# The opening of a two-layer attention kernel: who splits the first projections, who issues the first queries, and where three loads stand

## The reference

```python
# layer 0: causal self-attention plus attention to a context, 16 heads of 16 channels
q, k, v    = heads(xn @ Wq + bq), heads(xn @ Wk + bk), heads(xn @ Wv + bv)        # "s"
y          = softmax(causal(q k' / 4)) v
qc, kc, vc = heads(xn @ Wcq + bcq), heads(ctx @ Wck + bck), heads(ctx @ Wcv + bcv)  # "x"
x = x + (y + softmax(qc kc' / 4) vc) @ Wp + bp          # xn = layernorm(x)
x = x + bitlinear_ffn(layernorm(x))                      # weights rounded to -1, 0, 1
# layer 1: attention to the context ("f"), then an FFN with 8-bit weights and tokens
x = x + softmax(q k' / 4) v @ Wo + bo
x = x + int8_ffn(layernorm(x))
```

## Time and profile before

| | us |
|---|---|
| median of 3 runs | 1824.35 (1822.88 to 1830.0) |
| the profiled execution, its own time | 1824.27 |
| its span, from the first to the last instruction | 1822.5 |
| busy: PE 1643.0, DVE 1356.4, ACT 1151.3, POOL 663.0 | |
| mean granted TensorE clock | 0.953 of full speed |

### The profile page before, as it was taken

The page is one execution under the profiler, slowest core; times in us unless marked ns, Lnnn a source line. Parts: engine busy times, 40 slices in busy tenths (PEclk is TensorE's granted clock), DMA queues, the critical chain, the costliest instruction groups (busy, mean ns, idle before and its releaser), DMA issues.

```text
span 1822.5 us, 29171 instructions
## 1 busy us (share of the span) xinstructions
PE 1643.0 (90%) x10064; PEld 735.4 (40%) x10064; DVE 1356.4 (74%) x2549; ACT 1151.3 (63%) x2178; POOL 663.0 (36%) x915
## 2 busy tenths in 40 slices
PE   5898799998999999998999899998999988899677
PEld 1344345433543345433543344333544443333236
DVE  6667867788687877777777868877487687687287
ACT  1474585666665686667655675657655854765497
POOL 3435323551454134532454135523561242310140
PEclk7899999999999999999999999999999997999899
DMA  7444313323142323332242324233232231123123
GB/s 193 127 113 123 81 36 100 88 82 88 55 116 71 94 66 102 88 103 59 81 107 77 87 60 111 73 103 87 77 105 51 61 98 44 44 83 133 47 70 117
DMA packets 106947, 159.49 MB, mean 88 GB/s; under 512 B 20656, under 2 KB 83248, under 8 KB 106800
## 3 DMA queue, kind: packets, MB, share of 16 engines
q1 hardware_dynamic: 101904, 156.43, 30.8%
q10 hardware_dynamic: 4896, 1.18, 0.3%
HBM read 105.00 MB, written 51.38 MB: 86 GB/s over the span
## 4 chain that ended last, share of the span: by engine, by line
PE 57%; DVE 19%; ACT 11%; POOL 6%; issue 4%; DMA 2%; SPq 1%; ACTq 0%; DVEq 0%; POOLq 0%
PE acc L1495 12%; PE st L1481 11%; PE misc L1460 11%; DVE nmax L1258 8%; PE misc L1435 7%; PE misc L1407 4%; PE misc L1522 3%; ACT probs L991 3%; PE misc L1447 3%; ACT tail_h L1061 2%; ACT tail_h L1046 1%; PE misc L1536 1%; PE misc L1549 1%; PE st L1484 1%; POOL parts L876 1%
## 5 line engine op out<-in xcount | busy, mean ns | idle before, releaser
L1258 DVE TENSOR_REDUCE nmax<-misc 128x1 f32<-128x512 f32 (+2 forms) x1376 | 864.3, 672 | 294.1 <-PE misc L1460 169.3
L991 ACT ACTIVATE probs<-st 128x512 f32<-128x512 f32 (+3 forms) x1536 | 760.1, 551 | 371.8 <-PE st L1481 239.7
L1460 PE MATMUL misc<-stack 96*128 96x512 bf16 (+3 forms) x1536 | 536.1, 365 | 61.5 <-DVE nmax L1258 43.5
L1481 PE MATMUL st<-stack 99*128 99x512 bf16 (+3 forms) x1536 | 542.4, 364 | 36.3 <-ACT probs L991 30.9
L1481 PEld LDWEIGHTS st<-stack 99*128 99x128 bf16 x1536 | 148.9, 98 | 376.7 <-ACT probs L991 219.4
L1460 PEld LDWEIGHTS misc<-stack 96*128 96x128 bf16 x1536 | 152.1, 99 | 203.4 <-DVE nmax L1258 86.9
L870 POOL TENSOR_TENSOR parts<-qk,zero 128x512 bf16<-128x512 f32 x78 | 81.3, 1043 | 224.1 <-ACT qk L974 224.1
L1495 PE MATMUL acc<-probs,v_x 128*32 128x512 f32 x1152 | 159.8, 628 | 0.0
L1495 PE MATMUL acc<-probs,v_s 128*32 128x512 f32 (+3 forms) x1152 | 114.3, 469 | 0.1
L1484 PE MATMUL st<-mask_st,identb 128*128 128x128 bf16 x512 | 111.2, 220 | 0.0
L882 POOL TENSOR_TENSOR nparts<-nmax,zero 128x16 bf16<-128x16 f32 x96 | 22.2, 231 | 242.8 <-DVE nmax L1258 242.8
(11 more groups left out here) (261 smaller groups left out, 2094.5 us busy)
## 6 DMA issues: line engine op xcount, KB each, us to landing
parts_xk<-parts SPq DMA_DIRECT2D x54, 128.0 KB
parts_xq<-parts SPq DMA_DIRECT2D x54, 128.0 KB
stack<-parts_xq SPq DMA_DIRECT2D x36, 192.0 KB, 3.1
stack<-parts_xk SPq DMA_DIRECT2D x36, 192.0 KB, 3.6
parts_sk<-parts SPq DMA_DIRECT2D x48, 128.0 KB
parts_sq<-parts SPq DMA_DIRECT2D x48, 128.0 KB
stack<-parts_sq SPq DMA_DIRECT2D x32, 192.0 KB, 2.9
stack<-parts_sk SPq DMA_DIRECT2D x32, 192.0 KB, 3.4
```

What stands on the lines that cost most here:

```text
L991: act.activation(probs[:, j % P_SLOTS, c, T - w:], st_bank(n, 4 * j + c)[:, 0:w], ACT.Exp, scale=SCALE).then_inc(exp_done, 1)
L1258: dve.tensor_reduce(nmax[:, ring, first:first + NT * (len(cs) - 1) + 1:NT], src, AX.X, ALU.max, negate=True).then_inc(misc_free[slot], 1)
L1460: last = pe.matmul(o, stack[0:ROWS, r, 0, c, P * i:P * i + P], stack[0:ROWS, r, 1, c, 0:w], start=True, stop=not causal)
L1481: last = pe.matmul(o[:, 0:w], stack[0:AUG, r, 1, c, P * j:P * j + P], stack[0:AUG, r, 0, c, T - w:T], start=True, stop=not causal)
```

## The change

Six edits, all in the opening; nothing that is computed changes, and the number of matmuls doesn't either.

1. `first_qk`: all four first projections come ahead of the two settles. Between the settles now stand the stacks of the first two units, with `w_load` 0 behind the first of these; `w_load` 0 is taken out of its old place.
2. The first half (m = 0) of the keys and queries of sequence 0 is split by ACT and DVE in turn: ACT writes the first part straight from PSUM and then `qk`, DVE subtracts, ACT copies the second part, DVE subtracts the third. DVE does its four in the order keys, queries, keys, queries. The second half stays as it was (keys on POOL, queries on DVE).
3. ACT issues the three stores of those first queries itself, waits until they have landed, and issues the query loads of the first two units' stacks. SP keeps the keys.
4. SP's stores of the second half wait until the second settle, so that they come behind the stacks of the first two units and `w_load` 0.
5. `warm_up`: the turning of the first unit's maxima (`negmax_T`) stands after 5 of the second unit's 16 maxima matmuls, not after 9.
6. `turn(0)`: `w_load` 1 and `load0` 1 no longer stand ahead of the first unit. The cards of the first unit are now two empty ones, `w_load` 1, the projection with its settle, and `load0` 1 as the last.

```diff
@@ warm_up
-        second[:9] + [("negmax_T", us[0])] + second[9:]
+        second[:5] + [("negmax_T", us[0])] + second[5:]
@@ first_qk
-    return [x for m in range(KC) for x in [("project", b, p + "k", m), ("project", b, p + "q", m), ("settle", b, p, m)] +
-            [("stack", u) for u in us[2 * m:3][:2]]]
+    return [("project", b, p + w, m) for m in range(KC) for w in "kq"] + \
+        [x for m in range(KC) for x in [("settle", b, p, m)] + [("stack", u) for u in us[2 * m:3][:2]] + [("w_load", 0)] * (m == 0)]
@@ turn
-        return [("w_load", 1), ("load0", 1)] + slots(us[:1], project(0, "s"), 1, True) + \
+        return slots(us[:1], [None] * 2 + [("w_load", 1)] + project(0, "s") + [("load0", 1)], 1, True) + \
@@ BEFORE
-... + first_qk(0, "x", FIRST) + [("w_load", 0)] + [("v", 0, "x")] + \
+... + first_qk(0, "x", FIRST) + [("v", 0, "x")] + \
@@ who splits
-            return s.key[1] == 0 and s.args[0] == "xq"
+            return s.key[1] == 0 and s.args[0] == "xq" and s.args[1] == 1
+        def split_first(s):
+            return s.key[1] == 0 and s.args in (("xk", 0), ("xq", 0))
+        def part_order(w):
+            return (0, 1, 2) if w[1] == "q" else (2, 1, 0)
+        def queries_by_act(u):
+            return u in FIRST[:2]
@@ SP, project(s, late=False)
+                if s.key[1] == 0 and (s.args == ("xq", 0) or (w, m) in (("xk", 1), ("xq", 1)) and not late):
+                    return
@@ SP, settle
+                if s.key[1] == 0 and s.args == ("x", 1):
+                    for w in "kq":
+                        project(Step(("project", 0, "x" + w, 1), None), True)
@@ SP, stack_ (load_stack holds the three DMAs that stood here)
+                    if name == "k" or not queries_by_act(s.unit):
+                        load_stack(sp, s, w, name)
@@ ACT, project
+                if split_first(s):
+                    act.activation(parts[:, n.slot(QK_RING), part_order(w)[0], :], misc[misc_slot(s)][:, :], ACT.Identity,
+                                   bias=Bq[w][:, m:m + 1]).then_inc(qk_split[n.slot(QK_RING)], 1)
                 act.activation(qk[:, n.slot(QK_RING), :], misc[misc_slot(s)][:, :], ACT.Identity, ...
+                if s.key[1] == 0 and (w, m) == ("xq", 0):
+                    for w_ in ("xk", "xq"):
+                        r = s.ring("parts", ("project", 0, w_, 0)).slot(QK_RING)
+                        act.wait_ge(qk_split[r], 4 + 2)
+                        act.copy(parts[:, r, 1, :], qk[:, r, :]).then_inc(qk_split[r], 1)
@@ ACT, new settle and stack_
+                    act.wait_ge(qk_split[slots_["xq"]], 4 + 4)
+                    for a in range(PARTS):
+                        act.dma_start(qk_parts["xq"][a, :, 0:8, :].rearrange("d h t -> h d t"),
+                                      parts[:, slots_["xq"], a, :]).then_inc(parts_out[slots_["xq"]], 16)
+                    act.wait_ge(parts_out[slots_["xq"]], 96)
+            def stack_(s):
+                if queries_by_act(s.unit):
+                    load_stack(act, s, 0, "q")
@@ DVE, project
+                if s.key[1] == 0 and s.args == ("xq", 0):
+                    for half in range(2):
+                        for w in ("xk", "xq"):
+                            r = s.ring("parts", ("project", 0, w, 0)).slot(QK_RING)
+                            part = [parts[:, r, a, :] for a in part_order(w)]
+                            dve.wait_ge(qk_split[r], 4 + 1 + 2 * half)
+                            if half == 0:
+                                wait_misc_read(dve, s, 0, ("project", 0, w, 0))
+                            dve.tensor_tensor(part[2] if half else qk[:, r, :], qk[:, r, :], part[half],
+                                              ALU.subtract).then_inc(qk_split[r], 1)
```

More of the change, by code:

```diff
@@ L298 @@
 FIRST = turn_units(0)
-BEFORE = [("load0", 0), ("consts_load", 0)] + tokens0(0) + [("consts", 0)] + first_qk(0, "x", FIRST) + [("w_load", 0)] + [("v", 0, "x")] + \
+BEFORE = [("load0", 0), ("consts_load", 0)] + tokens0(0) + [("consts", 0)] + first_qk(0, "x", FIRST) + [("v", 0, "x")] + \
     warm_up(FIRST)[3:] + [("consts_rest", 0)]
@@ L645, in two_layers_kernel, with load_stack @@
         t_row, t_hsc, t_htot, t_end = sem("t_row"), sem("t_hsc"), sem("t_htot"), sem("t_end")
+        def load_stack(eng, s, w, name):
+            r, p, g = s.n.slot(STACKS), s.unit[1], s.unit[2]
+            src = parts_of(s.unit[0], p + name)[:, :, HU * g:HU * g + HU, :].rearrange("a d h t -> (a d) h t")
+            for row, first, k in ((0, 0, 3), (3, 0, 2), (5, 0, 1)):
+                if name == "k":
+                    first = PARTS - k
+                eng.dma_start(stack[D * row:D * (row + k), r, w, :, :],
+                              src[D * first:D * (first + k)]).then_inc(stack_landed[r], 16)
         def st_bank(n, k):
@@ L698, in load_mid, with project @@
                 sp.dma_start(xmid[:, :, :], batch_of(tokens, s.b.at())).then_inc(mid_in, 16)
-            def project(s):
+            def project(s, late=False):
                 n, (w, m) = s.ring("parts"), s.args
@@ L720, in stack_ @@
             def stack_(s):
-                r, p, g = s.n.slot(STACKS), s.unit[1], s.unit[2]
                 if s.n.base >= STACKS:
@@ L860, in project @@
             def project(s):
-                if split_early(s) or split_by_dve(s):
+                if split_first(s) or split_early(s) or split_by_dve(s):
                     return
@@ L865, in project @@
                 r, done = n.slot(QK_RING), n.round(QK_RING).times(4, 4)
-                order = (0, 1, 2) if s.args[0][1] == "q" else (2, 1, 0)
-                part = [parts[:, r, a, :] for a in order]
+                part = [parts[:, r, a, :] for a in part_order(s.args[0])]
                 wait_misc_read(pool, s)
@@ L973, in project, with settle @@
                 act.wait_ge(qk_split[n.slot(QK_RING)], n.round(QK_RING).times(4, 4).at())
+                if split_first(s):
+                    act.activation(parts[:, n.slot(QK_RING), part_order(w)[0], :], misc[misc_slot(s)][:, :], ACT.Identity,
+                                   bias=Bq[w][:, m:m + 1]).then_inc(qk_split[n.slot(QK_RING)], 1)
                 act.activation(qk[:, n.slot(QK_RING), :], misc[misc_slot(s)][:, :], ACT.Identity,
                                bias=Bq[w][:, m:m + 1]).then_inc(misc_free[misc_slot(s)], 1)
+                if s.key[1] == 0 and (w, m) == ("xq", 0):
[3 more added lines that the diff above has]
+                        act.copy(parts[:, r, 1, :], qk[:, r, :]).then_inc(qk_split[r], 1)
+            def settle(s):
+                if s.key[1] == 0 and s.args == ("x", 0):
+                    slots_ = {w: s.ring("parts", ("project", 0, w, 0)).slot(QK_RING) for w in ("xk", "xq")}
+                    act.wait_ge(qk_split[slots_["xq"]], 4 + 4)
[6 more added lines that the diff above has]
+                    load_stack(act, s, 0, "q")
             def negmax_T(s):
@@ L1034, in _ @@
             walk(act, dict(consts=consts, consts_rest=consts_rest, weights=weights, ctx_T=ctx_T, norm_T=norm_T, project=project, negmax_T=negmax_T, scores=scores,
-                           heads_copy=heads_copy, y_T=y_T, quant_T=quant_T, gelu=gelu, hid_peak=hid_peak, down_q=down_q,
+                           settle=settle, stack=stack_, heads_copy=heads_copy, y_T=y_T, quant_T=quant_T, gelu=gelu, hid_peak=hid_peak, down_q=down_q,
                            down_T=down_T))
```

## The result

The changed kernel takes 1842.94 us in the median (4 runs, 1841.86 to 1843.7) where the kernel before takes 1826.35 beside it (4 runs, 1822.88 to 1830.0): a ratio of 1.0093, 95% interval 1.0071 to 1.0114, slower by 16.6 us. In a later set of runs it was 1843.51 (9 runs) against 1826.04 (20 runs), ratio 1.0086 (1.0057 to 1.0115). The forecast was 1834.0, slower, with a range up to 1839.5: the direction is right, the size is too small, and the time lies outside the range.

What follows compares the result with a forecast made beforehand. PE's later work, moved by the opening, was taken as the bound. Sum: 1824.27 - 6.45 (earlier first score) + 1.7 (later projections) + 13.6 (context late beside it) + 0.9 (clock) = 1834.0 us, range 1828.0 to 1839.5.

Steps and rivals of the forecast that it cites:

- The bound and the place of the price: PE bounds the kernel; load0 1 behind the settle makes PE stand about 15 us at sequence 1's context.
- The first split: Opening: DVE subtractions take 0.69 us, ACT's first store at 20.0, last store landed at 24.7 against 26.7, gaining 2.0 us.
- The first stack: Opening loads on two queues: landed at 30.0 instead of 32.86, maxima start 2.9 us earlier (bounds 2.0 and 3.4).
- The first score: End of the first maxima: row landed by then, first score at 48.2 instead of 54.66, 6.45 us earlier.
- The bound for a late row: First score: if the maxima's row still took 6.79 us, landing at 49.1, the gain would be 5.0 us.
- the first score gains only the start: Rival at the first score: maxima's rows still land last, gain only 2.9 us, total 1837.6; chance 0.11.
- The third unit's stack: Opening, behind SP's late second-half stores: lands near 41, asked for at 48, price nothing with some 7 us of cover.
- From the first score to the context: Settle ends 32.0 + 1.7 us after the first score; context load issued, landing at 86.7 instead of 77.88.
- The clock: After PE's 15 us rest at the context it restarts at 1.2 GHz: +0.9 us (bounds -0.8 and +2.5).
- The sign that the prediction set itself: Prediction wrong if from 130 us on work lies less than 7 or more than 13 us behind before.
- The gain holds: Rival at the context: wait hidden if settle ends by 18.4 us after the first score, 1817.8 us; chance 0.07.
- Partly given back: Rival after the context: wait paid, up to 6 us come back at later PE stops, say 1829.5; chance 0.14.

Runs made afterwards that it cites:

- queries by SP: Changed kernel with load0 1 issued together with w_load 1 and the first two stacks' query loads back on SP: 1825.05 us (ratio 0.9986), second set 1820.86 us (0.9967).
- the changed kernel once more: The changed kernel run again unchanged beside the kernel before: 1843.51 us against 1826.04.
- the delayed one: Kernel before with 13.0 us more of memsets on DVE ahead of its first work: 1846.41 us, ratio 1.0102.

## Why the prediction was right in kind and wrong in size

**The bound and the place of the price: right.** `load0` 1 behind the settle makes PE, and with it DVE and ACT, stand at the context. The idle time forecast was about 15 us, and 15.08 was measured (15.14 in the second trace). Taking only this away takes the whole loss away (ratio 0.9992), and doing only this gives 1.0099.

**The first split: nearly right.** Subtractions of 0.69 and 0.70 us, as taken, and the first store from ACT at 20.4 (forecast 20.0). In the profiled execution PE gave the first queries at 16.92 instead of 15.95 us, 1.0 us late. That is no part of the change: the second trace of before has 16.92 as well, and the changed kernel's second has 16.01.

**The first stack: the step that failed.** "I take 30.0" stood between issuing (29.5) and moving the bytes (30.8); it landed at 33.44, 0.6 us later than before instead of 2.9 earlier. This term of the sum, with its bounds of 2.0 and 3.4, was mis-sized by 3.5 us; with the measured one the forecast would have been 1837.5, inside its own range. The upper bound assumed that the first unit's bytes would still take 6.1 us, as when only they were issued. They took 7.2 to 8.1 in the four traces with two queues, and 5.9 to 6.2 with one in the three that share the rest of the change. The rule of the Trainium skill (Trainium Kernel Development and Optimization, Key Constraints) that a second issuing engine only saves issue time was cited and then given no weight. The traces here go further: it gave less than that, a loss of 1.0 to 2.2 us. The stores, too, landed only at 26.25, not at 24.7: ACT takes 2.85 us for issuing three of them where I took SP's 1.8, so the last went out at 22.46 and not at 21.2, and it took 3.79 us to landing, not 3.45.

**The first score: right in its mechanism.** It follows the last maxima with no stop, as forecast: 51.71 = 33.49 + 18.2, where the forecast had 48.2 = 30.0 + 18.2. The gain is 2.95 us instead of 6.45. The whole difference of 3.5 is the first stack's. The row's last packets moved between 49 and 50 us, so it landed later than the 49.1 that the prediction named as a sign against itself, but it was also issued 3.5 us later (45.84, not 42.3), and PE needed it only at 51.71. (The bound for a late row should have been 5.3 by its own figures, 54.41 less 49.1, not 5.0.) The rival "the first score gains only the start" gave nearly the measured gain (2.9) by the wrong cause, which is luck; PE did not wait for the row of maxima. The third unit's stack, priced at nothing with some 7 us of cover, landed at 49.85 instead of near 41 and was asked for at 51.93: nothing was paid, with 2.1 us to spare.

**From the first score to the context: right.** Settle ended 33.9 us after the first score (forecast 32.0 + 1.7 = 33.7), and the load came 5.2 us behind it (4.8). PE went on 39.1 us after the first score, forecast 38.5.

**The clock: right for its place.** Lateness went from 12.95 at the context to 13.87 at the next stop by DVE (101.67, in the earlier trace rows 87.80): +0.92, forecast +0.9. Then a slow stretch of the kernel before at 88 to 94 us (granted clock 0.72) had no counterpart, and 1.2 came back: 12.7. So by 157 us the clock's part is -0.3 us, where +0.9 was forecast.

**The sum.** The forecast had 9.75, the trace has 12.7 at 157 us. The 3 us between are the first stack (+3.5), settle and load (+0.6), and the stretch just named (-1.2).

**The range.** It was built around the trace's own terms and left out how far executions of one kernel lie apart. In the sets above the kernel before ran from 1817.2 to 1835.7 us. Of its 73 executions in the four later sets, the 26 under 1825 us had a mean granted clock of 0.955 to 0.961, and the 36 over 1828 us one of 0.949 to 0.955. The trace on which the sum rested, 1824.27, was one of the quicker ones; medians were 1826.0 to 1829.5. A sum made on it is low by 2 to 5 us from the outset. The remaining 3.9 us between the lateness (12.7) and the difference of medians (16.6) are not settled. The interval of the ratio reaches down to 1.0071, 13.0 us, so they may be scatter: queries by SP differs from its lateness by 2.6 us one way in its first set and by 3.9 us the other way in its second (-3.1 against -5.7, -8.6 against -4.7). But the changed kernel once more (17.5 against 12.4) and the delayed one (20.4 against 15.3) came out on the same side, by 5.1 us each, so a loss that goes with a late start isn't ruled out. The sign that the prediction set itself, 7 to 13 us behind from 130 us on, held at 157 us and, in the first trace, not from 197 us on (13.9 to 19.3).

**The rivals.** "The gain holds" fell: its point was a settle done by 18.4 us after the first score, and it was done at 33.9. "Partly given back" fell as well: nothing but the 1.2 us came back. The third is dealt with above: its time, 1837.6, is the nearest to the measured one and still 5.3 us under it.

## What to carry to other kernels

Where one list orders the queues of all engines, moving a load behind a wait moves it behind everything for which that wait stands: look up who asks for the load, and when, before looking at what the move clears. In these traces a small DMA that a critical step needs landed in time when it was issued ahead of the large loads, and late when it came among them; each of two edits that change this order a little left the wait in place. Count lateness unit by unit against two traces of the same kernel, so that what is scatter isn't explained.

## What was not expected of the hardware

- The time at which TensorE's clock rises differs between executions of the same instructions. ACT copies the result of the first query projection at 15.95 us in one trace of the kernel before and at 16.92 in the other; with the versions of the changed kernel it was 15.45 to 17.00. In the changed kernel's first trace the weight loads of PE's projection matmuls are 0.85 us apart up to 15.6 and 0.43 from 16.3 on, while the table of windows has the granted clock as 1.00 for both stretches. The Trainium skill (TensorE: Matmul & The Clock Gate, The HAM clock gate) says that the chip's watch on activity runs freely, is not reset by a kernel, and that the point of change varies from run to run for that reason. These traces agree in that it varies, by 1.0 us between the two of the kernel before; they don't show the reason. The later steps go with the granted clock (105.7 us at 0.92 to 113.9 at 0.82 for one stretch of work), and the scatter of 1817 to 1836 us does for the most part (0.955 to 0.961 in the quick executions, 0.949 to 0.955 in the slow ones).
- 12 KB on ACT's queue took 6.0 to 9.5 us to land in the six traces in which SP had issued 1.5 MB or more of loads in the few us ahead of them, as in the earlier trace rows. In the trace of before none of its 51 packets moved up to 50 us, one did up to 52, and the other 50 came between 52 and 54.7, where the DMA view has

```profile
q1 hardware_dynamic: 543, 0.60, 111.0%
q10 hardware_dynamic: 50, 0.01, 2.6%
```

  The page DMA: Bandwidth & Descriptors of the Trainium skill (Queues, rings and completion order) has each DMA engine take the queues for which it has work in turn, packet by packet. By that alone the row would not wait, and here it does: no packet of it moves for the first 2.4 us. What holds it back ahead of the engines, its descriptors or its issue, the traces don't show.
- Two queues for the first two stacks landed the first 7.2 to 8.1 us after its first issue (four traces), one queue 5.7 to 6.6 us after it (nine traces), at the same number of bytes, although all was issued sooner.
